# Out-projection, norms and transposes of row tiles 0 to 6 moved into the loop of the first attention

## What is computed

```python
x = x + xattn(layernorm(x), ctx, ctx)   # 16 heads of 64, 512 keys per batch; its output is
                                        # layernorm(out @ Wo + bo + query) * gamma + beta
x = x + attn(layernorm(x))              # 16 heads of 32, 64 keys per batch, rotary positions
x = x + ffn(layernorm(x))               # 8 experts, top 2, 512 -> 2048 -> 512, exact gelu
```

## Time and profile before

| | us |
|---|---|
| median of 3 runs | 1711.19 (1710.65 to 1711.69) |
| span of the profiled execution | 1722.8 |
| loop of the first attention, PE | 75 to 956 |
| out-projection stage behind it | 956 to 1023 |
| second attention | 1023 to 1198 |
| experts | to the end |

### The profile page before, as it was taken

The page is one execution under the profiler, slowest core; times in us unless marked ns, Lnnn a source line. Parts: engine busy times, 40 slices in busy tenths (PEclk is TensorE's granted clock), DMA queues, the critical chain, the costliest instruction groups (busy, mean ns, idle before and its releaser), DMA issues.

```text
span 1722.8 us, 27504 instructions
## 1 busy us (share of the span) xinstructions
PE 1626.7 (94%) x10730; PEld 1369.6 (79%) x10730; DVE 1167.8 (68%) x1976; ACT 941.9 (55%) x1730; POOL 307.2 (18%) x258
## 2 busy tenths in 40 slices
PE   7999999999999999999999988995799999999987
PEld 6888888888888888888887766773688889889876
DVE  4377777777777777777777676774668549549852
ACT  5466666666566666666566434443556337336631
POOL 3201211011101111011100351554411002102101
PEclk9999999999999999999999999995899999999889
DMA  6601820111101110111011640113757428527721
GB/s 225 213 23 53 135 72 17 44 55 56 53 7 53 56 54 17 44 55 57 4 40 69 201 131 27 57 43 99 249 140 234 147 87 241 157 95 236 218 50 21
DMA packets 54106, 165.19 MB, mean 96 GB/s; under 512 B 10612, under 2 KB 10996, under 8 KB 53408
## 3 DMA queue, kind: packets, MB, share of 16 engines
q1 hardware_dynamic: 38032, 131.88, 22.4%
q0 software_dynamic: 15920, 31.19, 8.6%
HBM read 143.54 MB, written 55.64 MB: 116 GB/s over the span
## 4 chain that ended last, share of the span: by engine, by line
PE 85%; DVE 5%; ACT 3%; issue 3%; DMA 3%; POOL 1%; SPq 0%; ACTq 0%; POOLq 0%; DVEq 0%
PE psum L407 59%; PE psum L752 12%; PE psum L412 5%; PE psum L529 4%; PE psum L509 3%; ACT P L1382 2%; DMA raw<-in_W 2%; DVE Wh L831 1%; PE psum L683 1%; PE psum L611 1%; DMA ya<-residuals 0%; DMA raw<-in_Wv 0%; DVE hs L1177 0%; DVE P L1033 0%; DVE mx L1024 0%
## 5 line engine op out<-in xcount | busy, mean ns | idle before, releaser
L407 PE MATMUL psum<-ctx,Wk 128*128 128x512 f32 x1536 | 386.5, 400 | 0.0
L407 PE MATMUL psum<-Wv,ctx 128*128 128x512 f32 x1536 | 368.7, 389 | 0.0
L407 PEld LDWEIGHTS psum<-Wv,ctx 128*128 128x128 f32 x1536 | 288.3, 188 | 59.9
L407 PEld LDWEIGHTS psum<-ctx,Wk 128*128 128x128 f32 x1536 | 280.2, 189 | 56.0
L918 DVE SCALAR_TENSOR_TENSOR kT<-psum,bkc,kT 64x512 fp32r<-64x512 f32 x256 | 192.1, 750 | 169.3 <-ACT kT L1292 165.2
L407 PE MATMUL psum<-xgT,Wh 128*128 128x224 f32 (+5 forms) x1536 | 251.5, 317 | 13.8 <-issue 9.1
L407 PEld LDWEIGHTS psum<-xgT,Wh 128*128 128x128 f32 x1536 | 229.6, 197 | 31.7 <-issue 12.3
L752 PE MATMUL psum<-Wh,hs 128*128 128x512 f32 x981 | 244.3, 394 | 0.3 <-DVE hs L1177 0.3
L1302 ACT ACTIVATE Pr<-Pr,smn 128x512 f32<-128x512 f32 x128 | 92.8, 725 | 234.1 <-DVE smn L927 234.1
L1292 ACT ACTIVATE kT<-psum,bkc 64x512 fp32r<-64x512 f32 x256 | 175.2, 684 | 76.7 <-PE psum L407 73.0
L752 PEld LDWEIGHTS psum<-Wh,hs 128*128 128x128 f32 x981 | 180.2, 189 | 34.1 <-DVE hs L1177 0.8
(11 more groups left out here) (151 smaller groups left out, 1941.9 us busy)
## 6 DMA issues: line engine op xcount, KB each, us to landing
raw<-in_W SPq DMA_DIRECT2D x128, 512.0 KB, 4.2
expert_rows<-in_spare_rows SPq DMA_DIRECT2D x16, 1042.0 KB, 7.4
raw<-in_ctxT SPq DMA_DIRECT2D x32, 512.0 KB
xg<-expert_rows POOLq DMA_DIRECT2D x32, 256.0 KB, 5.0
low_parts<-Olo POOLq DMA_DIRECT2D x32, 128.0 KB, 2.4
oT<-low_parts SPq DMA_DIRECT2D x8, 512.0 KB, 4.5
out_x<-x SPq DMA_DIRECT2D x12, 256.0 KB
xs<-in_x SPq DMA_DIRECT2D x4, 512.0 KB, 6.6
```

What stands on the lines that cost most here:

```text
L407: mm = pe.matmul(dst, l, r, start=n == 0, stop=n == len(pairs) - 1)
```

## The change

- Project the keys first: the context's values are projected two steps behind the keys (project_v(n - 2)), not four ahead, and the four projections ahead of the loop are gone. Wk is loaded ahead of Wv. V has two buffers instead of three, queries are built for half a batch, every fourth step.
- The out-projection is cut in quarters of 6 matmuls, c_product(k) for k = 0 to 31, on bank 7. Quarters 0 to 27 (row tiles 0 to 6) run in steps 20, 24, ... 128. Wo is no longer kept: each quarter loads and splits its two blocks anew (wo_split_at: n % 4 == 2 from step 18 on). Every 16 steps the tile so finished is normalized, stored to the DRAM tensor x1_rows and turned (c_turn).
- Olo stays in SBUF; low_parts is gone.
- All loads of the loop behind number 13 use raw buffers 0 and 1 in turn, in the order in which they are split: the context's two at n % 8 == 3, the Wo blocks at n % 4 == 2, and at the end the attention weights (wa) and the last Wo blocks.
- The projections of tile 0 of the second attention are issued in steps 128 to 130. Tile 7's quarters 28 to 31, norms and turning stand in iterations 0 to 4 of the second attention.
- The rotary tables are loaded for one head and broadcast. x1 is read back from x1_rows. Many buffers have other places.

```diff
--- before.py
+++ after.py
...
+        NBURST = 4 * NT
+
+        def ctx_split_at(n):
+            return n % 8 == 3 and n < NS - 8
+
+        def wo_split_at(n):
+            return n % 4 == 2 and 18 <= n < NS
+
+        L_WQ, L_CTX0, L_WK, L_WV = 0, 4, 6, 10
+        number = {}
+        for n in range(NS):
+            if ctx_split_at(n):
+                for c in range(2):
+                    number["ctx", n // 8 + 1, c] = 14 + len(number)
+            if wo_split_at(n):
+                number["wo", (n - 18) // 4] = 14 + len(number)
+            if n == NS - 4:
+                for c in range(2):
+                    number["wa", c] = 14 + len(number)
+        for key in [("wa", c) for c in range(2, 6)] + [("wo", NBURST - 4), ("wa", 6), ("wa", 7)] + [("wo", NBURST - 4 + c) for c in range(1, 4)]:
+            number[key] = 14 + len(number)
+        L_E = 14 + len(number)
+        raw_of = [n if n < L_CTX0 else n % 3 if n < 14 else n % 2 for n in range(L_E)]
+        raw_of += [(n + L_E) % 3 for n in range(10)] + [n % 4 for n in range(2 * E * NI - 10)]
         raw_turn = [raw_of[:n].count(r) for n, r in enumerate(raw_of)]
...
+            def fetch_wo(k):
+                i = k % 4
+                fetch(wo_load(k), wo_in[:, 2 * i:2 * i + 2, :])
 
             def fetch_attention(t):
                 w, c = divmod(t, 2)
                 src = a[("aWq", "aWk", "aWv", "aWo")[w]].rearrange("(k p) n -> p k n", p=P)
...
+                fetch(wa_load(t), src[:, 2 * c:2 * c + 2, :])
+
+            def first_residual(t):
+                if t:
+                    sp.wait_ge(x1_done, t)
+                sp.dma_start(ya[:], residuals[0, t * P:(t + 1) * P]).then_inc(ya_in, 16)
+
+            def second_residual(t):
+                if t:
+                    sp.wait_ge(nxT_psum, t)
+                sp.dma_start(xc[:], residuals[1, t * P:(t + 1) * P]).then_inc(xc_in, 16)
+
+            for n in range(NS):
+                b, j = divmod(n, NJ)
+                if n == 1:
+                    sp.dma_start(residuals[1], a["x"]).then_inc(x_copied, 16)
+                if j == 0:
+                    sp.dma_start(lists[b * WIDE:(b + 1) * WIDE, :], a["spare_rows"]).then_inc(spares_in, 16)
+                if ctx_split_at(n):
+                    fetch_ctx(b + 1)
+                if wo_split_at(n):
+                    fetch_wo((n - 18) // 4)
+                if n == 18:
+                    sp.wait_ge(residual_added, 32)
+                    first_residual(0)
+                    second_residual(0)
+                elif n > 18 and n % 16 == 2:
+                    first_residual(n // 16 - 1)
+                elif n > 24 and n % 16 == 7:
+                    second_residual(n // 16 - 1)
+                if n == NS - 4:
+                    fetch_attention(0)
+                    fetch_attention(1)
+
+            for t in range(2, 6):
+                fetch_attention(t)
+            sp.wait_ge(v_psum, NS)
+
+            def fetch_bias(v):
+                sp.dma_start(absb[v][:], a[("abq", "abk", "abv", "abo")[v]].partition_broadcast(P)).then_inc(bias_in[v], 16)
+
+            def fetch_x1(t):
+                sp.wait_ge(x1_out, 16 * (t + 1))
+                sp.dma_start(x1[:, t, :], x1_rows[t * P:(t + 1) * P]).then_inc(x1_in, 16)
+
+            for v in range(3):
+                fetch_bias(v)
+            first_residual(NT - 1)
+            fetch_wo(NBURST - 4)
+            fetch_bias(3)
+            for t in range(NT - 2):
+                fetch_x1(t)
+            fetch_attention(6)
+            fetch_attention(7)
+            fetch_wo(NBURST - 3)
+            second_residual(NT - 1)
             sp.dma_start(brb[:], a["br"].partition_broadcast(P)).then_inc(r_in, 16)
             sp.dma_start(wrp[:], a["Wr"].rearrange("(k p) e -> p k e", p=P)).then_inc(r_in, 16)
-            residual(5)
             for dst, name in ((before, "before"), (ones, "ones"), (slot_from, "slot_from"), (row_of, "row_of")):
                 sp.dma_start(dst[:], a[name]).then_inc(e_in, 16)
...
+            fetch_x1(NT - 2)
+            for k in range(NBURST - 2, NBURST):
+                fetch_wo(k)
+            fetch_x1(NT - 1)
+            sp.wait_ge(c_psum, NBURST)
...
+                if u >= 4:
+                    pe.wait_ge(c_sum, u - 3)
+                if u >= 8:
+                    pe.wait_ge(nxT_lo, u // 4 - 1)
...
+            def c_product(k):
+
+                t, i = divmod(k, 4)
                 rows = slice(t * P, (t + 1) * P)
...
+                loaded(wo_load(k))
+                pe.wait_ge(o_lo, min(k + 4, NS // HALF))
+                if k > NBURST - 4:
+                    pe.wait_ge(nxT_lo, NT - 1)
+                    pe.wait_ge(c_sum, k)
+                low = Olo[(2 * t + i // 2) % 3]
+                products(bank[7], split_pairs([(Ohi[:, 2 * i + jj, rows], low[:, (2 * i + jj) % HALF, :]) for jj in range(2)],
+                                              [pair(Wo, slice(None), jj) for jj in range(2)])).then_inc(c_psum, 1)
...
+            for n in range(NS + 3):
+                if n < NS:
+                    project_k(n)
+                if 0 <= n - 1 < NS:
+                    scores(n - 1)
+                if 0 <= n - 2 < NS:
+                    project_v(n - 2)
+                if NS <= n:
+                    project(0, n - NS)
+                if n >= 6 and n % HALF == 2:
+                    weigh(n // HALF - 1)
+                if n >= 20 and n % 4 == 0:
+                    c_product((n - 20) // 4)
+                if n >= 37 and n % 16 == 5:
+                    c_turn(n // 16 - 2)
+                if 0 <= n - 2 < NS:
+                    turn(n - 2)
...
+                if i == 0:
+                    c_product(NBURST - 4)
+                    project(1, 0)
+                    c_turn(NT - 2)
...
+                if i == 1:
+                    c_product(NBURST - 2)
...
+                if i == 0:
+                    c_product(NBURST - 3)
...
+                if i == 1:
+                    c_product(NBURST - 1)
...
+            def c_add(k):
+                t, i = divmod(k, 4)
+                v.wait_ge(c_psum, k + 1)
+                if i == 0:
+                    v.wait_ge(ya_in, 16 * (t + 1))
                 else:
-                    v.wait_ge(low_out[u % 4], 16 * (u // 4))
-                v.tensor_tensor(Olo[u % 4][:], bank[7][:, 0:HALF * TB].rearrange("p (s q) -> p s q", s=HALF), hi, ALU.subtract).then_inc(o_lo, 1)
+                    v.wait_ge(c_sum, k)
+                v.tensor_tensor(ya[:], bank[7], ya[:], ALU.add).then_inc(c_sum, 1)
+                if i == 3:
+                    row_stats(ya[:], 2, ya_stat, t, (c_sum, k + 1))
...
+                if n >= 20 and n % 4 == 0:
+                    c_add((n - 20) // 4)
+                if n >= 33 and n % 16 == 1:
+                    c_scale(n // 16 - 2)
+                if n >= 34 and n % 16 == 2:
+                    c_shift(n // 16 - 2)
+                if n >= 37 and n % 16 == 5:
+                    nxT_low(n // 16 - 2)
...
+                if i == 2:
+                    c_scale(NT - 1)
+                if i == 3:
+                    c_shift(NT - 1)
...
+                if i == 0:
+                    c_shift(NT - 2)
+                    o_low(NS // HALF - 1)
+                    c_add(NBURST - 4)
+                if i == 4:
+                    nxT_low(NT - 1)
...
+            def wo_high(k):
+                if k:
+                    s.wait_ge(c_psum, k)
+                split_high(wo_load(k), Wo[0][:])
+
+            def wa_high(t):
+                w, c = divmod(t, 2)
+                if t == 0:
+                    s.wait_ge(v_psum, NS - NJ)
+                elif t == 2:
+                    s.wait_ge(k_psum, NS)
+                elif t == 6:
+                    s.wait_ge(o_psum, NS)
+                    s.wait_ge(v_done, NS)
+                split_high(wa_load(t), Wa[w][0][:, 2 * c:2 * c + 2, :])
...
+                    if n == 0:
+                        s.wait_ge(norm_out, 16)
+                    if ctx_split_at(n):
+                        if b:
+                            s.wait_ge(v_psum, n - 3)
                         ctx_high(b + 1)
                     s.wait_ge(k_psum, n + 1)
...
+                if wo_split_at(n):
+                    wo_high((n - 18) // 4)
+                if n == NS - 4:
+                    wa_high(0)
+                    wa_high(1)
+                if n == NS - 1:
+                    wa_high(2)
+                    wa_high(3)
+                if n == NS:
+                    wa_high(4)
+                    wa_high(5)
+                if n >= 36 and n % 16 == 4:
+                    nx_normal(n // 16 - 2)
+                if n >= 37 and n % 16 == 5:
+                    nxT_high(n // 16 - 2)
+            o_high(NS // HALF - 1)
...
+                if i == 0:
+                    wo_high(NBURST - 4)
+                    nx_normal(NT - 2)
+                    nxT_high(NT - 2)
+                    wa_high(6)
```

(62 more changed lines are left out.)

479 lines of the change are left out of this document (185 added, 294 removed).

## The result

The changed kernel takes **1822.6 us** (median of 4 runs, 1822.0 to 1829.2) against 1710.9 us of the kernel before: 1.066 times as long, 95% interval 1.064 to 1.068, +111.7 us. The forecast was 1784 with a range of 1740 to 1812. The direction and the place were right, the size was too small.

What follows compares the result with a forecast made beforehand. It took PE, busy 94% of the span, as the bound. Ends +2.6, stalls +51.2 and clock +19.5 gave +73.3 us, scaled 73, so 1784 us, with a range of 1740 to 1812.

Steps and rivals of the forecast that it cites:

- 13 stalls before the scores: First attention's loop, n = 19 to 115: PE waits 7 x 3.2 + 6 x 4.8 = 51.2 us.
- middle stage: Between loop and second attention: 93.06 us hold 72 us of PE work, so 21 us may go.
- The walk of the ring: Loop's two raw buffers: Wo split, POOL's low part, fetch, context split, kT; scores wait 3.2 or 4.8 us.
- The landing: Second context half's load in the loop: lands 3.4 us after issue; 4.3 at the other end, stalls then 63 us.
- C: Rival: the ring doesn't stall in the loop and the middle stage's idle time is saved, 1704 us; 10%.
- D: Rival: a second scores in the loop waits as well, 2 to 3 us more per event, 1816 us; 8%.
- E: Rival: the moves cancel, stalls of 1 us or less, 1711 us; 3%.
- The clock: PE behind each loop stall: half speed loses 1.5 us, 19.5 for all 13; ends 0 and 3.4 each (44).
- Rival B: In the loop: the stalls come but the clock stays, 1760 us; 22%.
- The ends: Start +1.1 us, middle stage -21, end of the loop +20, second attention +2.5: +2.6 in sum.
- Scaling by 0.993: Whole kernel: profiled span 1722.8 us is 0.7% over the median 1711.2, so the difference of 73.3 becomes 73.
- A: The forecast itself: ring stalls and clock in the loop, 1784 us; 57%.

Runs made afterwards that it cites:

- second profile: The kernel before, unchanged, run and profiled once more: 1711.9 us, its profile's span 1710.1 us.
- the split behind the keys: Changed kernel with ACT's two context splits moved behind the copies of the keys (kT), still ahead of Pr's copies: 1782.6 us, 1.042 of the kernel before.
- first profile: The kernel before, unchanged, in the profile that the prediction read: span 1722.8 us, 11.6 us over its median.
- filling the stalls: Changed kernel with PE running the next value projection once more, its result overwritten, ahead of the scores in the 13 stalls: 1801.1 us, 1.052 of the kernel before.
- the one-step-later kernel: Changed kernel with both halves of the next context split at n%8 = 4 instead of 3: 1715.4 us, 1.0037 times the kernel before.
- Wo's low part on DVE: Changed kernel with the low part of the Wo split of n%8 = 2 made by DVE instead of POOL: 1798.4 us, 1.051 of the kernel before.

## Why the prediction was wrong, point by point

The difference of the second profile of before and that of after is 1821.2 - 1710.1 = 111.1 us; at the start of the last projection it is already 1263.7 - 1152.3 = 111.4. It divides so:

| term | predicted | measured | from |
|---|---|---|---|
| 13 stalls before the scores | 51.2 | 70.7 | rows of the 13 events |
| half clock behind them | 19.5 | 34.2 | 104.9 - 70.7 |
| start, middle stage, end, second attention | 2.6 | 6.3 | 1158.6 - 1152.3 |
| sum | 73.3 | 111.2 | |

Of the 38 us between the two sums 19.5 are the stalls, 14.7 the clock and 3.7 the ends. The measured time lies 10.6 us above the range, and either of the two large terms alone, put right, would have brought the forecast only to 1803 or 1799.

- **The walk of the ring: right up to its last link, and that is the step that failed.** "PE ... the scores of 27, waits to 880.4" takes kT's low part as the last thing for which the scores wait. The code has two waits there, and I let the second go because in the trace of before it is always over first: Pr's addition runs while PE is still on the next keys. Behind a stalled ACT it comes last. ACT's Pr copies (1.21) and DVE's additions (1.41), partly beside each other, put 1.5 us on each event: 4.75 for 3.2 and 6.2 for 4.8, 19.5 us in sum. Read in the same trace only to the end of kT's low part, the 13 stalls would sum to 50.1 us, against 51.2 predicted. The bounds did not cover it, since for the stalls they varied the landing alone.
- **The landing** came within 0.5 us of the 3.4 taken (3.4 to 3.9, 3.6 in the mean), and right were the 13 events, their steps, the 1.5 us more where c_scale comes before (DVE's kT begins at 449.38, when c_scale's last statistic ends), and that the next keys are not late again. Rivals C, D and E are out. D's time of 1816 is the nearest to the measured one of all that the prediction gives, but by another way: no second scores waited.
- **The clock: 2.6 us for each event instead of 1.5.** The price was read behind the gap of 3.92 us alone. It was about right for stalls as short as predicted: 1.3 each with stalls of 2.9 to 3.2 and 4.6 in the run with the split behind the keys. In the changed kernel it was 2.0 to 2.4 behind stalls of 4.5 to 5.0, and 2.9 to 3.1 behind five of the six of 6.2 (1.4 behind the last). So the longer stall cost twice, once as waiting and once as clock. The trace of before already held a higher price: behind the gap of 4.47 us the clock stayed at 0.50 until 1045.4, for 4.5 us of work, so 2.2 lost, and I noted only that it was low. The second profile adds that one gap doesn't fix the price: behind the same gap of 3.92 us PE ran at 0.50 until 1028.2, so 2.9 us were lost where the first profile has 1.5. The upper end of 3.4 each was read from no row; the most that these traces show behind a stall of the loop is 3.1. Rival B is out for the stalls as they are, though its point is real: the five stalls of 2.9 to 3.0 us had no drop.
- **The clock as a cost of its own** was shown by filling the stalls: 28 us. Only 6 of the 34 would have been waited out anyway.
- **The ends.** The middle stage gave back what was read: 93.7 us long in the second profile for 72 of work, so 21.7 (21 predicted). The start cost 2.0 us (0.45 at the first scores, 1.55 at the context split of n = 3, which I had not looked at) instead of 1.1. End of the loop: 2.0, 4.4 and 7.8 us of waits for 4, 4 and 7.5, and some 4 us of clock, 18 for 20. Second attention: 9 us instead of 2.5, since I had neither the wait of 2.0 for tile 7's transposes nor the half clock behind both (4.6 us by the lengths of the rows behind them). -21.7 + 2 + 18 + 9 is 7.3, 1 us over what the landmark gives.
- **Scaling by 0.993** rested on the first profile's length, and moved the result by 0.5 us only. The 1745 and 1808 given for A and B with a landing of 3.4 to 4.3 don't come out of the landing, which gives 1760 to 1796; the rest is left to the ends without a sum.

The loads of Wo (32 blocks of 512 KB instead of 4, 14.7 MB more; 10 MB in all, 175.2 for 165.2, since the low parts no longer travel) were costed at nothing beyond the ring, and the one-step-later kernel bears that out: idle time and clock of PE in the loop are there those of the kernel before.

## What to carry to other kernels

Where a ring of buffers serves two kinds of load, ask which split stands right ahead of the one that needs the same buffer: here seven microseconds of distance, one figure in one condition, were worth 107 us. When an engine is going to be late, list every wait of each instruction behind it, also those that are never the last in the present trace; they all shift, and the last of them sets the stall. And price the clock behind a stall of PE as a range, from several rows of about that length and from more than one execution: the same wait cost 1.5 us in one and 2.9 in another.

## What the runs showed of the hardware

**Half clock by length of the idle time, in this loop.** From windows of 1 us around the 39 stalls of three kernels (the changed one, the split behind the keys, Wo's low part on DVE). Behind gaps of 2.9 to 3.0 us before the scores: full clock in all five cases. 3.1 to 3.9: half clock in eight of nine, for 3 to 7 us. 4.5 to 5.0 in the changed kernel: some 7 us at 0.50, about two of them still in the gap. 6.2: some 10 us in four of six, four of them in the gap. Gaps of 4.55 us in the kernel with the split behind the keys had only some 3 us, all of it behind the gap. So the length of the gap doesn't tell alone. Nor does the place: the gap of 3.92 us of the earlier trace rows, behind which the first profile is back at 1.00 at 1025, is there again in the second profile, and the clock is still 0.50 five microseconds on. The last row is of the first profile, behind the gap of 4.47 us (columns of rows 2):

```profile
1022.37 1.12 PE L412 MATMUL psum<-ident,nxc 128*128 128x128 f32 x4 [3.92 <-ACT nxc L1324]
1027.00:1028.00 1.00, 1.00 (x4) 0.71 (x4) 0.96 (x2) 0.00 (x0) 0.54 (x1) 0.50 0.00 0
...
1044.00:1045.00 1.00, 1.00 (x3) 0.77 (x3) 0.93 (x4) 0.00 (x0) 0.00 (x0) 0.50 0.03 8
```

The Trainium skill (TensorE: Matmul & The Clock Gate, HAM oscillation — how this bites in real kernels) describes half clock paid again behind each wait for a load. The 13 events of the changed kernel agree; behind the five gaps of 2.9 to 3.0 us there was none.

**A small DVE instruction beside a POOL split.** c_shift, 128x1, takes DVE 0.15 us, but 2.35 where POOL was splitting beside it (the kernel with the low part on DVE, with POOL's split; the last row is the same line in the changed kernel, where POOL was idle):

```profile
454.47 2.35 DVE L978 SCALAR_TENSOR_TENSOR rstd<-mv,rstd 128x1 f32<-128x1 f32 x1
454.32 2.49 POOL L1583 TENSOR_TENSOR ctx<-raw,ctx 128x1024 fp32r<-128x1024 f32 x1 [8.41 <-ACT ctx L1270]
...
456.19 0.15 DVE L978 SCALAR_TENSOR_TENSOR rstd<-mv,rstd 128x1 f32<-128x1 f32 x1
```

DVE's instruction and POOL's end within 0.01 us of each other, at 456.8, and DVE's takes 2.35 in all six cases of that kernel. The scaling of a 128x512 tile (c_scale, two instructions) likewise took 0.75 us each in the loop, and 2.1 and 2.7 beside POOL's splits at its end. DVE had room in this loop, so it cost nothing there; a move of POOL's work beside such instructions would have to be priced by it.
